# One extra bf16 product in front of each group of turns and each router product, in the four routing stages of a four-layer kernel

## The reference, cut to what matters

```
h      = layernorm(x)                       # [8192, 128]
scores = h @ router_w (+ router_b)          # [8192, E'], E' = 16, 8, 6 and 12
```

```
x = _layernorm(x + attn_out, ln1_g, ln1_b)
gp   = softmax(xt @ w_group + b_group)
elog = einsum('td,gde->tge', xt, w_expert) + b_expert
```

## Time and profile before

| | |
|---|---|
| median of 3 executions | 3397.09 us (3393.05 to 3399.75) |
| the profiled execution's own time | 3396.84 us |
| its span, first to last instruction | 3395.0 us |
| TensorE matmul busy | 2554.7 us (75%) |
| VectorE busy | 2189.5 us (64%) |
| ScalarE busy | 1594.0 us (47%) |
| granted TensorE clock, mean | 0.869 of full speed |
| stage `d` | from 406.0 us to 447.4 us |
| stage `m1` | from 1072.7 us to 1114.6 us |
| stage `m2` | from 2224.6 us to 2266.4 us |
| stage `m3` | from 3022.9 us to 3070.2 us |

### The profile page before, as it was taken

One profiled execution on the slowest core, in us unless ns is written; L12 is line 12 of the kernel. 1 busy time (PEld: TensorE's weight loads), 2 busy tenths in 40 slices (PEclk: granted clock), 3 DMA queues, 4 the chain that ended last, 5 costly groups with the idle time before them and its releaser, 6 DMA issues. The chain is left out here.

```text
span 3395.0 us, 71130 instructions
## 1 busy us (share of the span) xinstructions
PE 2554.7 (75%) x19941; PEld 1860.1 (55%) x19941; DVE 2189.5 (64%) x4872; ACT 1594.0 (47%) x3527; POOL 776.3 (23%) x1113
## 2 busy tenths in 40 slices
PE   3657759999897566999459999966567999972370
PEld 1334543459787333999237777766444666651260
DVE  5967875237687423776856666556977888863267
ACT  2545513332364233776636666632254777750253
POOL 0001100000000365555422222200151222203553
PEclk7899859999998688999679999958787999975695
DMA  3093000111371011222685555300095556500123
GB/s 99 0 253 100 31 13 23 32 45 51 63 122 56 29 43 47 70 69 63 212 184 70 69 68 68 47 1 0 0 262 66 69 69 75 72 33 23 59 76 104
DMA packets 316132, 240.86 MB, mean 71 GB/s; under 512 B 27068, under 2 KB 297836, under 8 KB 315692
## 3 DMA queue, kind: packets, MB, share of 16 engines
q1 hardware_dynamic: 288248, 202.91, 30.4%
q0 software_dynamic: 19072, 28.28, 2.9%
q10 hardware_dynamic: 8704, 8.39, 0.9%
HBM read 139.83 MB, written 96.51 MB: 70 GB/s over the span
## 5 line engine op out<-in xcount | busy, mean ns | idle before, releaser
L2562 ACT ACTIVATE h_pt<-h_ps 128x384 f32<-128x384 f32 (+1 forms) x1024 | 543.0, 544 | 279.1 <-PE h_ps L2471 143.8
L2311 DVE TENSOR_REDUCE h_nm<-h_ps 128x4 f32<-128x1024 f32 (+1 forms) x448 | 540.0, 1219 | 158.3 <-PE h_ps L2442 62.1
L1846 POOL DMA_INDIRECT results<-e_y,e_ykey x208 | 212.3, 1021 | 191.0 <-DVE e_y L1835 171.2
L1803 DVE TENSOR_SCALAR e_wt<-w 128x1156 f32 (+1 forms) x208 | 140.9, 678 | 174.6 <-PEq L1583 89.5
L2490 PE MATMUL h_ps_o<-h_pt,h_vp 128*32 128x256 f32 (+1 forms) x4096 | 246.8, 359 | 1.3 <-ACT h_pt L2562 1.3
L1893 ACT ACTIVATE e_hid<-e_ps_h,e_wt 128x128 f32<-128x128 f32 x688 | 201.9, 369 | 21.9 <-PE e_ps_h L1867 14.3
L1867 PE MATMUL e_ps_h<-e_hT,e_wt 128*128 128x128 f32 x1376 | 197.4, 284 | 14.5 <-ACT e_hT L1888 7.9
L1875 PE MATMUL e_ps_o<-e_wt,e_hid 128*128 128x128 f32 x1376 | 194.9, 280 | 8.5 <-ACT e_hid L1893 4.9
L2476 PE MATMUL h_ps<-h_sq,h_sk 128*128 128x256 bf16 x1024 | 193.8, 275 | 9.2 <-ACT h_pt L2562 4.4
L1656 POOL DMA_INDIRECT sorted_rows<-e_row,e_pos x128 | 123.2, 963 | 301.4 <-DVE e_row L1635 243.8
L2413 PE MATMUL h_ps<-h_sk,h_sq 128*128 128x256 bf16 x1024 | 160.9, 282 | 37.8 <-DVE h_identb L2293 35.5
(11 more groups left out here) (449 smaller groups left out, 6283.5 us busy)
## 6 DMA issues: line engine op xcount, KB each, us to landing
h_sk<-k_stack SPq DMA_DIRECT2D x192, 128.0 KB
q_stack<-p_parts SPq DMA_DIRECT2D x64, 256.0 KB, 3.3
h_sq<-q_stack SPq DMA_DIRECT2D x64, 256.0 KB
sorted_rows<-pad SPq DMA_DIRECT2D x26, 520.0 KB, 11.6
e_xt<-sorted_rows SPq DMA_DIRECT2D x104, 130.0 KB
e_got<-results SPq DMA_DIRECT2D x24, 512.0 KB, 5.1
k_stack<-p_parts SPq DMA_DIRECT2D x32, 384.0 KB, 3.2
b_tz<-ktab SPq DMA_DIRECT2D x32, 256.0 KB, 7.1
```

The costliest lines, as they stand in the source:

```text
L1803: dve.tensor_scalar(wt[j % 4][:, :], w[:, :, :].rearrange("p e w -> p (e w)")[:, ds(at, wc)], 1.0, None, ALU.mult).then_inc(e_w.sem, 1)
L1846: gp.indirect_dma_start(ys[:, :], bass.IndirectOffsetOnAxis(ap=key[m // 4][:, m % 4:m % 4 + 1], axis=0), y[m][:, :], None).then_inc(return ...
L2311: dve.tensor_reduce(to, got, AX, ALU.max, negate=True).then_inc(s["mx"].sem, 1)
L2562: act.activation(pt[g % 2][:, j, :], ps_2[:, h % 2, 0:SW], ACT.Exp, scale=scale).then_inc(s["ex"].sem, 1)
```

## The change

A bf16 tile `dense` of 128x512 is filled once per stage by DVE from the first four tiles of the stage's source. TensorE waits for it. Then, ahead of each group of four turns and ahead of each router product, it does one product of `dense`'s first 128 columns (as weights) with all 512 columns of `dense`, into a PSUM bank that nothing reads. That is 32 products per stage and 128 in the program.

```
@@ def route
             with ExitStack() as st:
+                dense = sb(f"{tag}_dense", [P, U], BF16, stack=st)
+                ps_d = bank(f"{tag}_ps_d", st)
+                k_dense = n_chain[0] + 1
...
                     @block.vector
                     def _(dve):
+                        link(dve, dve.tensor_copy(dense[:, :].rearrange("p (t d) -> p t d", t=UT), src[:, 0:UT, 0:D]))
+
...
                     @block.tensor
                     def _(pe):
+                        pe.wait_ge(chained, k_dense)
+
+                        def kept_warm():
+                            pe.matmul(ps_d[:, 0, :], dense[:, 0:P], dense[:, :], start=True, stop=True)
+
                         def turn(n, j, r):
+                            kept_warm()
                             turn_tiles(pe, fr.tps, ps_t[:, j, :], nrm[j], UT, fr.nrm.now(n, 1), fr.hT.ago(n, 1, S))
 
                         def project(n, j, r):
+                            kept_warm()
                             pe.wait_ge(*fr.hT.now(n, 1))
                             pe.wait_ge(*kept.ago(n, 1, S))
```

## The result

| | before | after |
|---|---|---|
| median | 3397.09 us (5 executions, 3392.1 to 3400.9) | 3438.37 us (5, 3416.4 to 3442.0) |
| ratio after / before | | 1.0114 (95%: 1.0087 to 1.0140) |
| span of the profiled execution | 3395.0 us | 3414.6 us |

The account below looks back on a forecast made before the run. TensorE at 1.2 GHz bounds `d`, `m1`, `m2`, with DVE nearly level in `m3`. Growth of 13.8 us in `d`, 13.2 each in `m1` and `m2`, 10.1 in `m3`, together 50 on 3397, gives 3447 us; range 3396 to 3456.

Parts of the forecast that it names:

- The clock stays low in the loop: TensorE in all four routing stages stays at 1.2 GHz; sum 3447 us, chance 0.48.
- the train: Opening of `d`, `m1`, `m2`: product, turns, product, turns, product without a gap, one dense stretch of 2.6 us.
- rival B: Added products lift and hold the clock in all four loops; 3367 us, chance 0.09 shared with three stages high.
- Rival A: Openings lift some of `d`, `m1`, `m2` by chance: one 3424 us (0.25), two 3401 (0.12), three 3378.
- The unit: Each low-clock loop unit grows by 0.86 us, 0.43 per product, from 2.45 to 3.31 us.
- The cast: Ahead of all norming in each stage, uncovered: 0.75 us of a range 0.4 to 1.0; four are 3.0 us.
- `m3` grows least: Stage `m3` grows by 10.1 us, less than the others, because TensorE had waited for DVE there.
- Rival C: Products hide nothing, their weight load in the open: 1.16 us a unit, 3464 us, chance 0.06 with its like.
- The reason why the loop stays low: Loop too thin to lift: for 1.4 of 3.31 us, router products of 6 to 16 columns stream almost nothing.

Follow-up runs that it names:

- e1: Changed kernel without the two extra products ahead of the turns of units 0 and 1 in all four stages; 3398.76 us, ratio 1.0120.
- e12: The kernel of e1 measured again in the third series; 3444.88 us, ratio 1.0132.
- e3: Changed kernel with no extra products in stage `m3`, its cast kept; median 3390.9 us, ratio 1.0039.
- e11: The changed kernel itself measured again in the third series; median 3420.98 us, ratio 1.0060.
- e4: Changed kernel with two extra products in each place instead of one; 3344.76 us, ratio 0.9964.
- e5: Kernel before plus float32 streams ahead of and opening `d`, `m1`, `m2`, cast on ACT, two 512-column products per unit there; 3360.32 us, ratio 0.9895.
- e6: As e5, but with no bf16 products in the loop and no cast; 3374.9 us, ratio 0.9941.
- e2: Changed kernel with three extra products instead of one ahead of the turns of units 0 and 1; 3336.5 us, ratio 0.9933.
- e9: e7 with no product and no cast in `d`, and three extra products around unit 1's turns in `m1` and `m2`; 3364.82 us, ratio 0.9893.
- e10: e9 with streams in every statistics block of the program; 3363.62 us, ratio 0.9898.
- e8: As e7, with the one product of 256 columns instead of 512; 3375.5 us, ratio 0.9944.
- e7: As e5, but one 512-column product per unit, ahead of the turns, none ahead of the router product; 3369.3 us, ratio 0.9907.

## Why the prediction was right, point by point

**The clock stays low in the loop: right.** Without the train no stage rose in 8 executions of e1 and e12, 24 openings. With it, 15 of 78 openings rose (1 of 15 in the first measurement, 5 of 30 in e3, 9 of 33 in e11, all by groups of times). If the loop itself did the lifting at that rate, 24 misses in a row would have a chance of 0.81 to the power of 24, 0.6%, taking openings as independent. So the loop's two products per unit did not raise the clock, and rival B falls at this dose; the `m3` of e4 shows that four can, in its one profiled execution. That the median itself fell among the executions with no stage lifted is in part luck: the median of e11 has one lifted.

**Rival A, the opening lifts by chance: right in kind and size.** A lifted stage was to be 23 us cheaper and its units 1.7 us. Measured: 54.43 - 31.19 = 23.2 us, and 1.67 us. The 23 is closer than its parts, whose errors make up for each other: `m1` low was to grow by 13.2 us against before, and `m2`, its like, grew by 11.5; `m1` high was to gain 9.5, and gained 11.7. The middles of the groups of e3 and e11 are 21 to 26 us apart. The forecast gave 0.46 to some stage rising. It did in one of the first five executions, in four of ten of e3 and in seven of eleven of e11.

**The unit: 3.23 us, not 3.31.** This is the main term that was mis-sized. Ahead of the router product the cost is the 0.43 us forecast. Ahead of the turns 0.35 is left: the turns follow 0.38 us after the product, and the open weight load of before is gone. I had this as the lower end (0.37) and chose the upper. Over 14 units and four stages that is 14 x 4 x 0.08 = 4.5 us of the 6.5 by which the sum was high (50 against 43.5).

**The cast: 0.43 us, 0.46 to the start of the norming, not 0.75.** 1.2 us over four stages. The row of 384 columns with 0.736 was the nearest in kind and misled; the shortest of the range was right. The rest, some 0.8 us, must lie in openings and tails; I did not split it.

**`m3` grows least: right.** +8.5 us, the smallest, where the sum had 10.1. It stayed low throughout, its unit bounded by TensorE at 3.22 us:

```profile
3044.98 1.72 PE L936 MATMUL m_ps_l<-pack,m_hT 128*128 128x12 f32 x8
3048.20 1.72 PE L936 MATMUL m_ps_l<-pack,m_hT 128*128 128x12 f32 x8
```

**Rival C fell:** the product's weight load is hidden, at 0.15 us beside the turns (419.16 in the timeline of `d`).

**The reason why the loop stays low was only half right.** I argued from thin columns in the loop. e5 (three stages) and the `d` of e6 show that a loop can hold the high level that it did not reach by itself. So it matters where it starts. My reading, as in the prediction, is that at 1.2 GHz a unit takes 2.45 us and at 2.4 GHz 1.28, so the same columns come twice as close; that is argued and not shown by a run of its own. It isn't sure to hold either: `m3` in e2, where TensorE waits for DVE, fell back with the same two products a unit, and the bare loop fell in three of its five stages (`m1` and `m2` of e6, `d` of e9).

**Left open.** Why `d` held in e6 and e10 and fell in e9, where each is known from one profiled execution. One thing differs in the traces: in e6 and e10 the clock was 1.00 all through the statistics, kept from the stage before, while in e9 it had been lost and was 0.65 in the window from 404 us, and in the `m1` and `m2` of e6, which fell too, it came up only as the statistics ended. But `m1` of e8 came in high as `d` of e6 did, with more in its loop, and fell, so this is a lead and no rule. e6 ahead of `d`, and e8 ahead of `m1`:

```profile
400.00:406.00 6.00, 3.64 (x14) 1.69 (x12) 4.29 (x17) 1.54 (x2) 0.00 (x0) 1.00 0.00 0
```

```profile
1050.00:1058.00 8.00, 3.73 (x12) 1.80 (x12) 5.75 (x23) 1.54 (x2) 0.00 (x0) 1.00 0.00 0
```

Also open: which instant decides whether an opening rises, since the trains of `d` and `m1` agree to 0.01 us; why the share of lifted openings differs between the three measurements, which may be chance; and whether a stream at the start alone, with the changed kernel's own cast on DVE, would do as well as e5.

## What to carry to other kernels

Before adding work to raise TensorE's clock, find out at which level the stage starts: the products in this loop cost 0.78 us on top of each 2.45 us unit at the low level, and never raised it by themselves; they held what something else had raised. Put the stream where TensorE is idle anyway, ahead of the stage, and leave only as much in the loop as keeps it (e5: -36 us, with all three stages high in its profile, where the change as made costs +41 or +21, by the luck of its openings). When the times of one kernel fall in groups one stage's gain apart, count the groups and read them against the profile; a median over them depends on luck, as the changed kernel's 3438 and 3421 us show.

## What the runs showed of the hardware that was not expected

- A stage of float32 turns and 16-column router products kept 2.4 GHz for 24 us (e6), and in another run fell after 10 us with TensorE busy 4.00 of 4.00 us (e9). The busy share of a window doesn't tell the level.
- Two stages with waits of 0.15 and 0.40 us in their openings and one 512-column product a unit fell to 1.2 GHz (e7); with three more products in the opening four of four stayed up (e9, e10). The products' own effect and that of the waits are not told apart.
- A 128x512 float32 to bf16 cast from SBUF to SBUF took 0.43 us on DVE, less than the 0.69 of a two-operand pass over as many columns.
- The kernel before took 3359.76 us on one chip and 3397 to 3400 on the others. The routing stages are alike there (54.43 us for a low `d`). From the end of `m1` to the start of `m2` e1 took 1082.3 us and the changed kernel 1109.7 on the chip of the first measurement, with the same instructions there, so 27 of the 37 us lie in that stretch. The granted clock over it is 0.93 in e1 and 0.91 in the changed kernel; what else differs is open.
